# Attention projections and the MLP's second product with tokens on the partitions

## The reference

```python
c_proj = silu(c) @ W_mod + b_mod           # per sequence: shift_a, scale_a, gate_a, shift_m, scale_m, gate_m
q, k, v = split((_ln(x) * (1 + scale_a) + shift_a) @ W_qkv + b_qkv)
x = x + gate_a * (softmax(q k^T / sqrt(8)) v @ W_proj + b_proj)
q_c = _ln(x) @ W_qc + b_qc;  k_c, v_c = split(_ln(context) @ W_kvc + b_kvc)
x = x + (softmax(q_c k_c^T / sqrt(8)) v_c @ W_cproj + b_cproj)
h = gelu((_ln(x) * (1 + scale_m) + shift_m) @ W_mlp1 + b_mlp1)
x = x + gate_m * (h @ W_mlp2 + b_mlp2)
x = router_block(x, cond, ctx)             # not touched by the change
```

## Time and profile before

| | us |
|---|---|
| median of 3 runs (lowest to highest) | 562.56 (562.55 to 564.73) |
| the profiled execution, device time | 563.06 |
| its span, from first to last instruction | 561.2 |
| busy: PE, DVE, ACT, POOL | 529.0, 433.5, 380.5, 276.2 |

### The profile page before, as it was taken

One profiled execution on the slowest core, in us unless ns is written; L12 is line 12 of the kernel. 1 busy time (PEld: TensorE's weight loads), 2 busy tenths in 40 slices (PEclk: granted clock), 3 DMA queues, 4 the chain that ended last, 5 costly groups with the idle time before them and its releaser, 6 DMA issues.

```text
span 561.2 us, 16447 instructions
## 1 busy us (share of the span) xinstructions
PE 529.0 (94%) x6175; PEld 384.4 (68%) x6177; DVE 433.5 (77%) x1271; ACT 380.5 (68%) x889; POOL 276.2 (49%) x296
## 2 busy tenths in 40 slices
PE   6988999999999999999999989998999999999995
PEld 5745666666566665666676756665788788888885
DVE  4778889788989889888887667767586786786565
ACT  6537778587787886878787685555754864864862
POOL 5637849569498686888860413224124124124100
PEclk9989999899999999999999999999999999999998
DMA  4665635634254343543330001001011011010000
GB/s 133 153 181 137 179 100 151 139 94 106 61 137 120 79 125 81 132 117 100 82 79 4 2 23 36 1 20 37 3 39 56 23 35 56 23 38 14 20 20 19
DMA packets 52939, 41.47 MB, mean 74 GB/s; under 512 B 6369, under 2 KB 52226, under 8 KB 52866
## 3 DMA queue, kind: packets, MB, share of 16 engines
q1 hardware_dynamic: 50792, 36.72, 24.9%
q10 hardware_dynamic: 2074, 3.77, 2.4%
HBM read 12.16 MB, written 2.10 MB: 25 GB/s over the span
## 4 chain that ended last, share of the span: by engine, by line
PE 63%; DVE 15%; POOL 7%; DMA 5%; issue 4%; ACT 4%; SPq 2%; ACTq 0%; DVEq 0%; POOLq 0%
PE PS L958 31%; PE PS L1833 7%; PE PS L1799 5%; PE PS L1885 4%; DVE NM L1613 3%; PE PS L1897 3%; PE PS L994 2%; DMA Qs<-MT 2%; PE PS L1817 2%; PE PS L1855 2%; PE PS L1890 2%; SPq L1343 2%; DVE r_T L933 2%; DVE r_R L936 1%; PE PS L1877 1%
## 5 line engine op out<-in xcount | busy, mean ns | idle before, releaser
L1613 DVE TENSOR_REDUCE NM<-PS 128x4 f32<-128x512 f32 x256 | 163.3, 681 | 30.0 <-PE PS L1799 29.4
L1499 ACT ACTIVATE PR<-PS 128x512 f32<-128x512 f32 x256 | 139.7, 600 | 27.0 <-PE PS L1817 26.4
L1799 PEld LDWEIGHTS PS<-Ks,Qs 64*128 64x128 bf16 x1024 | 57.3, 94 | 53.8 <-DVE NM L1613 28.7
L1799 PE MATMUL PS<-Ks,Qs 64*128 64x128 bf16 x1024 | 83.4, 218 | 5.6 <-DVE NM L1613 3.8
L1817 PE MATMUL PS<-Qs,Ks 64*128 64x128 bf16 x1024 | 83.6, 218 | 3.9 <-DMA Qs<-MT 3.3
L1833 PE MATMUL PS<-PR,Va 128*32 128x128 f32 x2048 | 83.3, 281 | 0.0
L744 ACT ACTIVATE r_HID<-PS,ANC 128x128 f32<-128x128 f32 x224 | 62.4, 378 | 18.5 <-PE PS L958 18.5
L655 POOL TENSOR_TENSOR m_veps<-m_mv,m_eps 128x4 f32<-128x4 f32 x16 | 3.6, 225 | 129.7 <-DVE m_mv L820 129.7
L1833 PEld LDWEIGHTS PS<-PR,Va 128*32 128x32 f32 x2048 | 48.5, 110 | 20.2 <-ACT PR L1499 6.9
L1817 PEld LDWEIGHTS PS<-Qs,Ks 64*128 64x128 bf16 x1024 | 57.1, 94 | 7.5 <-DMA Qs<-MT 3.8
L958 PE MATMUL PS<-r_NXS,r_WNS 128*128 128x512 f32 x168 | 52.6, 421 | 0.0
(11 more groups left out here) (198 smaller groups left out, 1110.1 us busy)
## 6 DMA issues: line engine op xcount, KB each, us to landing
Qs<-Qp SPq DMA_DIRECT2D x96, 128.0 KB
Ks<-Kp SPq DMA_DIRECT2D x90, 128.0 KB
CTXG<-in_ctx SPq DMA_DIRECT2D x8, 256.0 KB, 3.9
r_CTX<-in_ctx SPq DMA_DIRECT2D x8, 256.0 KB, 2.9
r_CTXT<-in_ctxt SPq DMA_DIRECT2D x8, 256.0 KB, 3.3
out<-X SPq DMA_DIRECT2D x8, 256.0 KB, 2.3
X<-in_x SPq DMA_DIRECT2D x7, 256.0 KB, 4.5
W<-in_weights ACTq DMA_DIRECT2D x2, 855.0 KB
```

Source lines behind the costliest of these rows:

```text
L1499: nc.scalar.activation(PR[:, u, :], T_BANK[u % 2][:, :], ACT.Exp, scale=SCALE)\
L1613: nc.vector.tensor_reduce(out=NM[:, c.b // 2, c.second, u // 2, u % 2 * 4:u % 2 * 4 + 4, 0], in_=S_BANK[score_bank(c, u)[0]][:, :].rearran ...
L1799: last = nc.tensor.matmul(S_BANK[bank][:, j * P:(j + 1) * P], Qs[c.stack][rows, lo + j, cols], Ks[c.stack][rows, lo + j, cols], start=True ...
```

## The change

The three products are turned round: the tokens' side becomes the stationary operand, block by block of 128 tokens, and the weights stream, so that tokens come out on the partitions and can be added to X straight from the bank. `yt_s`, `yt_c` and `turn_back` go, and so do YT and the reads into it. Gates and biases, no longer per-partition scalars, become rows repeated over all partitions:

- In round 0 a new fill, `gain`, makes gate_a, gate_m and both bias rows for the 32 sequences (PE, then four DVE instructions), and SP stores them to a DRAM tensor, `gains`.
- For each group, SP loads two repeated 128x512 rows, GS, before `proj_s`. POOL multiplies W_proj by the gate row into WG (`gain weights`), which `proj_s` streams, and adds the gated bias row to X. PE's `proj_s` waits for the first (semaphore gain_used), DVE's addition for both.
- POOL adds the cross-attention's bias CB to X behind ln_x's normalisation (`gain cross`).
- In the MLP, SP loads two rows G, POOL adds the bias row to X (`bias`), DVE multiplies the bank by the gate row and adds to X.
- In the setup, two of four modulation products, two bias products, and their ACT and DVE instructions go.

```diff
+def proj_steps(t, g):
+    return ([(t - 11.0, "gain", "load", g, 0), (t - 5.5, "gain", "weights", g, 0)]
+            + fill_steps(t, "proj_s", g, (1, t + 0.1)))
 def norm_steps(t, name, g):
+    if name == "ln_x":
+        return [(t, "norm", name, g, 0), (t + 0.05, "gain", "cross", g, 0)]
     return [(t, "norm", name, g, 0)]
...
-            + fill_steps(26.0, "proj_s", i + 2, (0, 26.1), (1, 26.2))
-            + fill_steps(29.0, "yt_s", i + 2, (1, 29.1)))
+            + proj_steps(26.0, i + 2))
...
-        steps += (fill_steps(10.0, "proj_s", 2 * i - 1, (0, 10.1), (1, 10.2))
-                  + fill_steps(12.0, "yt_s", 2 * i - 1, (1, 12.1)))
+        steps += ([(0.1, "gain", "load", 2 * i - 1, 0), (5.5, "gain", "weights", 2 * i - 1, 0)]
+                  + fill_steps(10.0, "proj_s", 2 * i - 1, (1, 10.1)))
...
+                elif ev[:2] == ("gain", "load"):          # SP
+                    g = ev[2]
+                    if g == 0:
+                        sp.wait_ge(gains_stored, 16)
+                    else:
+                        sp.wait_ge(gain_used, 2 * g)
+                    for at, row in enumerate((0, 2)):
+                        sp.dma_start(GS[:, at, :], gains[row:row + 1, g * GT:(g + 1) * GT].to_broadcast([P, GT]))\
+                            .then_inc(gains_in, 16)
...
+                elif ev[:2] == ("gain", "weights"):       # POOL
+                    pool.wait_ge(gains_in, 32 * (g + 1))
+                    pool.wait_ge(ln_done[0], g + 1)
...
+                    nc.gpsimd.tensor_tensor(WG[:, :].rearrange("p (b h) -> p b h", b=GB),
+                                            w("proj").unsqueeze(1).to_broadcast([P, GB, P]),
+                                            GS[:, 0, :].rearrange("p (b h) -> p b h", b=GB), ALU.mult)\
+                        .then_inc(gain_used, 1)
+                    nc.gpsimd.tensor_tensor(x, x, GS[:, 1, :], ALU.add).then_inc(gain_used, 1)
+                elif ev[:2] == ("gain", "cross"):         # POOL
...
+                    nc.gpsimd.tensor_tensor(x, x, CB[:, :].unsqueeze(1).to_broadcast([P, GB, P]), ALU.add)\
+                        .then_inc(x_biased, 1)
...
-                elif name == "read" and ev[1] in ("yt_s", "yt_c"):          # DVE
+                elif name == "read" and ev[1] in ("proj_s", "proj_c"):
                     dve.wait_ge(bank_filled[name], g + 1)
+                    if name == "proj_s":
+                        dve.wait_ge(gain_used, 2 * g + 2)
+                    else:
+                        dve.wait_ge(x_biased, g + 1)
                     nc.vector.tensor_tensor(x, GROUP_BANK[:, :], x, ALU.add).then_inc(bank_read[name], 1)
...
                     elif name in ("proj_s", "proj_c"):                      # PE
                         pe.wait_ge(o_stored, last_core.n + 1)
-                        last = nc.tensor.matmul(GROUP_BANK[:, :], w(("proj", "cproj")[KIND[name]]), OgT[KIND[name]][:, :],
+                        if name == "proj_s":
+                            pe.wait_ge(gain_used, 2 * g + 1)
+                        for b in range(GB):
+                            last = nc.tensor.matmul(GROUP_BANK[:, b * P:(b + 1) * P],
+                                                    OgT[KIND[name]][:, b * P:(b + 1) * P],
+                                                    WG[:, b * P:(b + 1) * P] if name == "proj_s" else w("cproj"),
+                                                    start=True, stop=True)
...
             elif name == "second":                                          # PE, MLP
...
-                product(SECOND_BANK[par][:, :], w("mlp2", k * P, P), H[:, k, :], start=k == 0, stop=k == 3)\
-                    .then_inc(second_done, 1)
+                for b in range(GB):
+                    last = product(SECOND_BANK[par][:, b * P:(b + 1) * P], H[:, k, b * P:(b + 1) * P],
+                                   w("mlp2", k * P, P), start=k == 0 and b == 0, stop=k == 3 and b == GB - 1)
+                last.then_inc(second_done, 1)
...
             elif name == "gate":                                            # DVE, MLP
...
+                nc.vector.tensor_tensor(WG[:, :], SECOND_BANK[par][:, :], G[par][:, 0, :], ALU.mult).then_inc(gated, 1)
...
+                nc.vector.tensor_tensor(x, WG[:, :], x, ALU.add).then_inc(x_added, 1)
```

More of the change, by code:

```diff
@@ L217, in round_steps @@
     elif i == 0:
-        steps = [e for e in regular_steps(0) if e[2] not in ("xt_s", "proj_s", "yt_s", "v1")]
+        steps = [e for e in regular_steps(0) if e[2] not in ("xt_s", "proj_s", "v1") and (e[1] != "gain" or e[2] == "cross")]
         steps += (fill_steps(0.2, "xt_s", 2, (0, 0.3), (1, 2.1))
@@ L385 @@
     ("first", 0, 0), ("second", -1, 0), ("first", 0, 1), ("second", -1, 1),
-    ("turn_back", -2, 0), ("norm", 2, 0), ("first", 0, 2), ("first", 0, 3),
+    ("gains", 0, 0), ("norm", 2, 0), ("first", 0, 2), ("first", 0, 3), ("bias", 0, 0),
     ("second", -1, 2), ("gelu", 0, 2), ("second", -1, 3), ("gelu", 0, 3), ("gate", -1, 0),
@@ L535, in mlp_and_router @@
     XTS = [rb(f"m_XTS{k}", [P, 2, GT], F32R) for k in range(2)]
+    G = [rb(f"m_G{k}", [P, 2, GT]) for k in range(2)]
     reused.close()
-    attended = bank_read["yt_c"]
+    attended = bank_read["proj_c"]
     GROUP_BANK = PS[6]
@@ L555, in mlp_and_router @@
     gated = sem("gated")
-    turned_back = sem("turned_back")
+    gains_loaded = [sem(f"gains_loaded{k}") for k in range(2)]
     x_added = sem("x_added")
@@ L637, in body, with mlp @@
                              X[:, bass.ds(g * GT, GT)].rearrange("p (b h) -> p b h", b=GB)).then_inc(out_done, 16)
+        def mlp(name, g, k, par, pair):
+            if name == "gains":
+                if g < 2:
+                    sp.wait_ge(shifted_done, 4 * NCORE)
+                else:
+                    sp.wait_ge(gated, g - 1)
+                    sp.wait_ge(x_biased, NG + g - 1)
+                for at, row in enumerate((1, 3)):
+                    sp.dma_start(G[par][:, at, :], gains[row:row + 1, g * GT:(g + 1) * GT].to_broadcast([P, GT]))\
+                        .then_inc(gains_loaded[par], 16)
         def rest():
             sp.wait_ge(attended, NG)
-            rest_of_groups(sp, lambda *step: None, body)
+            rest_of_groups(sp, mlp, body)
             sp.wait_ge(out_done, 16 * NG)
-        return {}, rest
+        return {"mlp": mlp, "between": lambda: between_cores(mlp)}, rest
     def gpsimd_programs(pool):
@@ L1162, in build_block @@
         expt = sb("expt", [P, 1])
-        YT = [sb(f"YT{k}", [P, GT]) for k in range(2)]
+        WG = sb("WG", [P, GT])
+        GS = sb("GS", [P, 2, GT])
+        gains = nc.dram_tensor("gains", [4, B * P], F32).ap()
         PS = [stack.enter_context(nc.psum_tensor(f"PS{k}", [P, 512], F32)) for k in range(8)]
@@ L1181, in build_block @@
         ln_mv = [sem(f"ln_mv_{k}") for k in kinds]
-        ln_var = [sem(f"ln_var_{k}") for k in kinds]
         ln_rstd = [sem(f"ln_rstd_{k}") for k in kinds]
```

188 lines of the change are left out of this document (78 added, 110 removed).

## The result

The changed kernel takes 596.6 us (median of 4, 594.7 to 598.3) against 563.2 before: ratio 1.059, 95% interval 1.054 to 1.063. The forecast of slower was right, 576.5 was not, and 596.6 lies outside the range. The profiled execution has a span of 596.5 against 561.2, which is +35.3.

The account below looks back on a forecast made before the run. PE was taken as the bound, busy 529.0 of 561.2 us. The terms 15.8+1.2+1.1-2-2.2 gave +13.9 on the profiled 563.06, so 577.0, and 576.5 for the median; range 563 to 584.

Parts of the forecast that it names:

- The loop: Rounds 0 to 4: `proj_s` waits for POOL's gated weights, delaying scores, maxima and the next ln_x statistics; +15.8 us.
- POOL's run: POOL's dense work from ln_x's veps to the weights' end: 31.0, 31.0, 28.76, 25.48 us in rounds 1 to 4.
- my 1.5: POOL's time over DVE's for a 128x512 addition, from trace rows of 1.04 and 0.684.
- The clock behind the stalls: PE's half clock after three new stalls of 5 us and more at `proj_s`: 0.4 each, +1.2 us.
- two ways of 12.50 and 12.10 us: Times before the change from `proj_s`'s start to the next ln_x veps, with and without half clock.
- V: The start of ln_x's veps on POOL, where POOL's dense run of a round begins.
- The row at 104 us: Profile before, 104 to 106 us: granted clock 0.50 behind a PE stall; `proj_s` took 2.08 against 1.12.
- the clock falls in every stall: Rival: each PE stall at `proj_s` loses about 1.3 us, not 0.4; +4, 581 us, between 577 and 587; chance 0.12.
- The start: Setup and round 0's `gain` fill: removed and added work cancel; 0, between -1.5 and +1.5 us.
- Rounds 5 to 7: Cross bias in POOL's run in round 5, +1.1; removed turns and ACT read against five POOL additions, -2 us.
- the -2 for the turns: Rounds 5 to 7: turns back and an ACT read leave the path, against five POOL additions; between -4.2 and 0.
- The MLP: Per group the turn back goes, 0.44, and four chunks cost 0.16 more: -0.28 a group, -2.2 us over eight.

Follow-up runs that it names:

- no_wait: Changed kernel, POOL's work in place, but PE and DVE's addition don't wait for it; self-attention projection's gate and bias left out; 573.2 us, ratio 1.016.
- stall_filled: Changed kernel with 1 to 5 unused PE products ahead of the waits for gated weights of groups 0, 2, 4, 5 and 6; 591.7 us, ratio 1.047.
- mlp_swapped: Changed kernel with only PE's and ACT's MLP order changed: second's third product between first's third and fourth; 596.4 us, ratio 1.058.
- two_buffers: Changed kernel with cross bias and all weights but the first group's outside POOL's dense run, second buffer for GS and WG; 569.5 us, ratio 1.012.
- gain_behind_turn: Changed kernel with two weight buffers, weights early, MLP order swapped, gain fill before round 0 behind the maxima's turn; 563.4 us, ratio 1.000.

## Why the prediction was right in its direction and wrong in its size

**The loop: right.** The weights behind POOL's run make `proj_s` wait (23.5 us), the wait returns through DVE's statistics in the next round, and without it 24.8 us of these rounds go (no_wait).

**POOL's run: the added operations were longer.** They took 1.26 to 1.28, not 1.04, and the four of round 1 lengthened its run by 5.07, not 4.48; the four runs became 1.9 us longer than forecast. The row that I took as nearest has one operand of four values a partition, each repeated over 128 columns; the added ones read new fp32 values from both operands along the row. A nearer row stood in the trace of the kernel before, in the MLP and router, with two whole fp32 operands:

```profile
L668 POOL TENSOR_TENSOR r_NXS<-r_NX,r_NXS 128x512 fp32r<-128x512 f32 x8 | 10.1, 1268 | 0.6
```

At 1.26 against 0.684 on DVE the factor is 1.8, if with other operands. The Trainium skill (GPSIMD Engine Reference, "Performance versus the Vector engine") gives about 2; the measured 1.8 is nearer to that than my 1.5 was.

**The clock behind the stalls: the step that failed.** The prediction put "three new stalls of 5 us and more" at 0.4 each, 1.2 in all, from two ways of 12.50 and 12.10 us. Measured against the forecast, the ways from the weights to the next V are 7.9 us longer in rounds 1 to 4, 6.7 above the 1.2 allowed, and 2.4 longer in round 0. stall_filled shows that most of it is the clock: 1.5 to 2.1 us a stall, and some 7 in all. The row at 104 us came behind a shorter gap (1.34 us) and was back at full clock after some 3 us, with DVE in work; behind the stalls of 2.0 to 6 us at the end of rounds 0 to 4 everything waits for PE, and PE runs at half clock for 3.5 to 6 us. That is nearly the rival "the clock falls in every stall", which the forecast priced at +4 and gave 0.12. Behind the two stalls of 1.7 us for the odd groups the granted clock stayed at 1.00, so that not every stall did it; behind the five at the rounds' ends it fell to 0.50. The rule of the Trainium skill named there (TensorE: Matmul & The Clock Gate, "HAM oscillation — how this bites in real kernels"), bursts that start at half clock behind idle gaps, agrees with these five. With this step alone put right (9.1 us more) the sum would have come to some 586, still above the range; the start, rounds 5 to 7 and the MLP, each put near nothing or below it, make up most of the rest.

**The start: an assumed wash that wasn't.** The setup's savings and the `gain` fill were set at 0, within 1.5. The rstd of round 0 ends 2.5 us later than before (69.75 against 67.26; in the execution of mlp_swapped, with the same attention part, at 68.51). The chain of waits shows PE's three kinds of products of the fill and DVE's four instructions in it one after the other:

```profile
38.90 1.06 PE PS L1917 x4
39.95 0.43 PE PS L1919 x2
40.38 0.74 PE PS L1921 x2
41.15 0.29 DVE CB L1680
41.44 0.19 DVE GS L1681
41.62 0.34 DVE GS L1682
41.99 0.42 DVE GS L1685
...
42.45 2.09 PE PS L1896 x2
```

3.5 us from 38.90 to 42.41, since the next fill (L1896) wants the same bank. A third of it is DVE's read, which the prediction counted as if it lay beside other work. The setup's savings came, too: the first scores start at 23.86, before at 25.02, with 0.3 of it from an earlier load of x. That the fill makes the start late is read from the chain alone; no run that moved it brought V1 back.

**Rounds 5 to 7: sign wrong.** -0.9 was forecast (+1.1 and -2), +2.9 measured. POOL's run is on the chain of waits in two long pieces, 248 to 266 us and 286 to 309, with three cross additions in them (1.27 each) where one was counted. The later two, from the chain:

```profile
289.46 1.27 POOL X L1440
290.73 1.01 POOL Kp L1469
...
306.98 1.27 POOL X L1440
308.26 1.01 POOL Kp L1469
```

With them and group 7's weights out of the run (two_buffers and the three runs built on it) the stretch is 1.3 to 1.6 us shorter than before, so the -2 for the turns was about right and POOL's share was the error.

**The MLP: sign wrong, small.** -2.2 was forecast, +1.8 measured to the end. The turn back was counted as PE time on the path; it stood in a wait for ACT's gelu, which now shows (mlp_swapped: from 7.2 us a group to 6.81 and 7.11). The whole time did not change by that swap, so that the cause of the 4.0 is shown for these groups only.

In sum, of the 21.4 us between the forecast's +13.9 and the +35.3 of the span: POOL's operations 1.9, the way behind the stalls 9.1, the start 2.5, rounds 5 to 7 3.8, MLP and router 4.0. What is not settled: whether the excess of the ways that stall_filled leaves (0.2 to 0.9 us in rounds 0 and 2 to 4) is DVE starting empty or the 1.36 of its read coming off only in part, and why V1 stays 3.5 us late in gain_behind_turn.

## What to carry to other kernels

Before giving an engine more work because it is idle half of the time, find the dense run inside which the new work will stand and who waits for its end; a place a few instructions earlier or later, in the idle stretch, was worth 19 us here, and 27 with a second buffer. Price a new stall of PE with the half clock behind it (1.5 to 2.1 us each here), not by a row where the pipeline stayed full. And work taken off an engine on the critical path gains nothing where it stood in a wait for another engine.

## What the runs showed of the hardware

POOL's TENSOR_TENSOR of 128x512 took 1.04 us where one operand was a value repeated over 128 columns or more, 1.16 with an fp32 and a bf16 tile, and 1.26 to 1.31 where both operands brought fp32 values along the row (two tiles, or a tile and a block of 128 columns repeated). The load of a repeated row of DRAM to all partitions landed in 4.5 us for 256 KB, against 3.7 for plain rows in the same trace, so the feared factor of two did not come:

```profile
GS<-gains SPq DMA_DIRECT2D x16, 256.0 KB, 4.5
...
CTXG<-in_ctx SPq DMA_DIRECT2D x8, 256.0 KB, 3.7
```
